# A graph network's projection on TensorE, with its operands swapped: the copied sums held, the weights streamed

## The reference

```python
# layer 0: every edge has 9 coefficients (edge_weight1, edge_attr_3, edge_attr_5)
msg[lo] += einsum('io,eik->eok', W[idx], einsum('ijk,ei,emj->emk', CG[le, ln, lo], sh[le], feats[ln]))
x = x + segment_sum(msg, dst)
# layer 1: 16 bases per edge, weighted by its relation and an attention value, and a self loop
x_hat, y_hat = h[src] @ A1_w.T + A1_b, h[dst] @ A2_w.T + A2_b + rel_emb[etype]
a = tanh(relu(sum(x_hat * y_hat, -1) / sqrt(32)))
msg = einsum('eb,ebo->eo', w_comp[etype], einsum('ei,bio->ebo', h[src], weight))
curr = h[src[last_e]] @ self_loop_weight
x = x + relu(where(in_deg > 0, segment_sum(a * msg, dst) + curr, 0))
```

## Time and profile before

| | us |
|---|---|
| median of 3 runs | 3294.89 |
| lowest and highest | 3294.35, 3296.32 |
| the profiled execution | 3295.84 |
| its span on the core | 3294.0 |
| PE busy in the span | 2972.4 |
| DVE busy | 2602.5 |
| POOL busy | 2414.9 |
| PE's weight loads busy | 2392.0 |
| ACT busy | 895.1 |

### The profile page before, as it was taken

The page is one execution under the profiler, slowest core; times in us unless marked ns, Lnnn a source line. Parts: engine busy times, 40 slices in busy tenths (PEclk is TensorE's granted clock), DMA queues, the critical chain, the costliest instruction groups (busy, mean ns, idle before and its releaser), DMA issues.

```text
span 3294.0 us, 108331 instructions
## 1 busy us (share of the span) xinstructions
PE 2972.4 (90%) x41934; PEld 2392.0 (73%) x41934; DVE 2602.5 (79%) x3897; ACT 895.1 (27%) x1910; POOL 2414.9 (73%) x2546
## 2 busy tenths in 40 slices
PE   2999999999999999999789999999999999899997
PEld 2777777777777777777677777777777777777776
DVE  7777777777777777777678888888888888888886
ACT  1111111111111111111344444444444444444342
POOL 6777777777777777777377777777777777777774
PEclk9999999999999999999789999999999999999998
DMA  4111111111111111111233333333333333332331
GB/s 138 28 28 28 28 28 28 27 28 27 28 27 29 27 29 27 29 27 29 67 55 58 55 59 59 57 56 59 58 57 56 59 58 58 55 58 54 58 57 40
DMA packets 220288, 150.94 MB, mean 46 GB/s; under 512 B 122954, under 2 KB 201083, under 8 KB 219901
## 3 DMA queue, kind: packets, MB, share of 16 engines
q0 software_dynamic: 81312, 41.79, 12.3%
q1 hardware_dynamic: 138013, 100.79, 12.3%
q10 hardware_dynamic: 576, 2.40, 0.2%
HBM read 136.54 MB, written 8.22 MB: 44 GB/s over the span
## 4 chain that ended last, share of the span: by engine, by line
PE 32%; POOL 9%; issue 5%; DVE 4%; DVEq 1%; DMA 0%; ACT 0%; POOLq 0%; ACTq 0%
PE ps L609 17%; POOL xg L541 9%; PE ps L634 5%; PE ps L675 4%; PE ps L622 3%; DVE scratch L960 2%; PE ps L657 1%; PE ps L572 1%; PE ps L645 1%; DVE Z L1044 0%; DMA xg<-h_table,idx 0%; DVE aggT L1062 0%; DVEq L960 0%; DVE blocks L951 0%; DVEq L1062 0%
## 5 line engine op out<-in xcount | busy, mean ns | idle before, releaser
L541 POOL DMA_INDIRECT xg<-h_table,idx x2541 | 2404.1, 946 | 844.1 <-issue 758.9
L609 PE MATMUL ps<-h,blocks 128*128 128x448 f32 x8190 | 1803.0, 372 | 237.5 <-DVE scratch L960 213.4
L609 PEld LDWEIGHTS ps<-h,blocks 128*128 128x128 f32 x8190 | 1501.3, 188 | 458.5 <-issue 324.1
L1044 DVE TENSOR_TENSOR Z<-coef,ps 128x864 f32<-128x864 f32 (+1 forms) x522 | 734.4, 1448 | 16.6 <-DVE ps L985 0.2
L951 DVE TENSOR_TENSOR blocks<-scratch,ps 128x896 fp32r<-128x896 int16 x585 | 630.1, 1077 | 34.4 <-PE ps L609 34.4
L675 PE MATMUL ps<-Z,xg 128*32 128x32 f32 (+3 forms) x25008 | 507.8, 215 | 8.3 <-DVE Z L1044 7.9
L675 PEld LDWEIGHTS ps<-Z,xg 128*32 128x32 f32 x25008 | 403.9, 110 | 93.0 <-issue 70.2
L1062 DVE TENSOR_TENSOR aggT<-aggT,ps 64x128 f32 (+1 forms) x262 | 74.1, 283 | 485.1 <-PE ps L657 478.4
L960 DVE SCALAR_TENSOR_TENSOR scratch<-ramp_sb,scratch,ps 128x448 f32<-128x448 f32 x585 | 396.7, 678 | 7.8
L830 ACT ACTIVATE p_left<-ps 96x128 f32<-96x128 f32 (+2 forms) x262 | 64.6, 246 | 1189.3 <-PE ps L645 1140.8
L965 DVE TENSOR_REDUCE xg<-scratch 128x32 f32<-128x448 f32 x585 | 362.8, 620 | 20.2
(11 more groups left out here) (105 smaller groups left out, 1109.4 us busy)
## 6 DMA issues: line engine op xcount, KB each, us to landing
xg<-h_table,idx POOLq DMA_INDIRECT x2541
rows_b<-typ_short SPq DMA_DIRECT2D x130, 258.0 KB
scratch<-q_short SPq DMA_DIRECT2D x260, 96.0 KB
rows_b<-dst_short SPq DMA_DIRECT2D x130, 126.0 KB
coef<-in_edge_dram SPq DMA_DIRECT2D x130, 54.0 KB
att_tab<-p_table SPq DMA_DIRECT2D x393, 8.1 KB
p_table<-Z SPq DMA_DIRECT2D x8, 297.0 KB, 3.9
X<-in_x_dram SPq DMA_DIRECT2D x7, 224.0 KB, 4.6
```

The lines of the kernel that those rows point to most:

```text
L541: pool.indirect_dma_start(xg[:, g.q, t - g.s * J, :], None, h_table[n], bass.IndirectOffsetOnAxis(ap=idx[:, t:t + 1], axis=0)).then_inc(L. ...
L609: last = pe.matmul(found_ps[b], blocks[:, b, c, :], h_2[:, a, c], start=(c == 0 and a == 0), stop=(c == NCH - 1 and a == 1))
L1044: dve.tensor_tensor(Z[:, b, js, 0:C * WN].rearrange("p j (c n) -> p j c n", n=WN), coef[:, js, :].unsqueeze(3).broadcast_to([P, k, C, WN]) ...
```

## The change

The projection swaps its operands. The copied sums `G_sb` of one half, 96 slots wide, now stand in the array, and the weights stream (64 columns in layer 0, 32 in layer 1). The result has slots on partitions at once and goes to `o_ps`. So there is no `turn`, no `oT_ps`, no `copy_oT` and no semaphore for them. Since a half fills the array, the chunks are gone through once per half: 2 x 3 matmuls of 64 columns instead of 3 of 192 in layer 0, 2 x 5 of 32 instead of 5 of 192 in layer 1. On ACT `copy_o` waits for the projection itself, and stands ahead of the attention of gs[1], where the two copies stood behind it. `place_rows` stays after the 8th tile.

```diff
@@ -198,9 +198,8 @@
 
         G_ps = ps[:, 0:2, :]
         ex_ps = ps[:, 2:4, :]
-        oT_ps = ps[0:2 * F, 4, :]
-        o_ps = ps[0:HW, 4, 2 * HW:2 * HW + 4 * F].rearrange("p (h o) -> p h o", h=2)
-        win_ps = ps[0:3 * F, 4, 2 * HW + 4 * F:2 * HW + 4 * F + P]
+        o_ps = ps[0:HW, 4, 0:4 * F].rearrange("p (h o) -> p h o", h=2)
+        win_ps = ps[0:3 * F, 4, 4 * F:4 * F + P]
         found_ps = [ps[:, 5 + b, 0:MC * F].rearrange("p (f m) -> p f m", f=F) for b in range(2)]
         S_ps = ps[:, 7, 0:J * WN].rearrange("p (j n) -> p j n", j=J)
         iota_ps = ps[:, 7, J * WN:J * WN + P]
@@ -295,9 +294,8 @@
         flat = p_left[:].rearrange("p m k -> p (m k)")
         at = 2 * CQ[1] * HW
         G_sb = flat[:, 0:at].rearrange("p (c h w) -> p c h w", c=CQ[1], h=2)
-        oT_sb = flat[0:2 * F, at:at + 2 * HW].rearrange("p (h w) -> p h w", h=2)
-        o_sb = flat[0:HW, at + 2 * HW:at + 2 * HW + 4 * F].rearrange("p (h o) -> p h o", h=2)
-        at += 2 * HW + 4 * F
+        o_sb = flat[0:HW, at:at + 4 * F].rearrange("p (h o) -> p h o", h=2)
+        at += 4 * F
         one_hot = flat[:, at:at + J * P // 2].bitcast(BF16).rearrange("p (j e) -> p j e", e=P)
         q_rows = coef1[:].rearrange("p b j c -> p (b j c)").bitcast(I16)[0:PS, 0:2 * NPM * P]
         span = squares[0:1].rearrange("p b m f -> p (b m f)")[:, 0:NG]
@@ -368,8 +366,6 @@
                 self.summed = sem(f"summed{n}")
                 self.G_set = sem(f"G_set{n}")
                 self.projected = sem(f"projected{n}")
-                self.oT_set = sem(f"oT_set{n}")
-                self.turned = sem(f"turned{n}")
                 self.o_set = sem(f"o_set{n}")
                 self.placed = sem(f"placed{n}")
                 self.added = sem(f"added{n}")
@@ -627,23 +623,14 @@
                     hh, w = g.halves()
 
                     pe.wait_ge(L.G_set, g.order())
-                    wait(pe, L.oT_set, g.order() - 1)
+                    wait(pe, L.o_set, g.order() - 1)
                     wait(pe, L.added, g.order() - 1)
-                    for c in range(cq):
-                        rows = P if c < cq - 1 else F
-                        last = pe.matmul(oT_ps[0:no, 0:hh * w], weights[0:rows, c, :], G_sb[0:rows, c, 0:hh, 0:w],
-                                         start=(c == 0), stop=(c == cq - 1))
+                    for h in range(hh):
+                        for c in range(cq):
+                            rows = P if c < cq - 1 else F
+                            last = pe.matmul(o_ps[0:w, h, 0:no], G_sb[0:rows, c, h, 0:w], weights[0:rows, c, :],
+                                             start=(c == 0), stop=(c == cq - 1))
                     last.then_inc(L.projected, 1)
-
-                def turn(g):
-                    hh, w = g.halves()
-
-                    pe.wait_ge(L.oT_set, g.order())
-                    wait(pe, L.o_set, g.order() - 1)
-                    pe.nop().then_inc(L.turn_go, 1)
-                    for h in range(hh):
-                        last = pe.transpose(o_ps[0:w, h, 0:no], oT_sb[0:no, h, 0:w], ident[0:no, 0:no])
-                    last.then_inc(L.turned, 1)
 
                 def place_rows(g):
 
@@ -678,8 +665,6 @@
                         if j == g.nj - 1:
                             last.then_inc(L.summed, 1)
                         if back and j == min(g.nj, J // 3) - 1:
-                            turn(back)
-                        if back and j == min(g.nj, 2 * J // 3) - 1:
                             place_rows(back)
 
                 def step(gs):
@@ -693,7 +678,6 @@
                     if gs[1]:
                         sum_edges(gs[1], gs[2])
                     elif gs[2]:
-                        turn(gs[2])
                         place_rows(gs[2])
 
                 def one_pass(k):
@@ -816,16 +800,9 @@
                     act.activation(to[0:F, :, cq - 1, :], bank[0:F, :, cq - 1, 0:w], ACT.Copy)
                     act.activation(to[:, :, 0:cq - 1, :], bank[:, :, 0:cq - 1, 0:w], ACT.Copy).then_inc(L.G_set, 1)
 
-                def copy_oT(g):
+                def copy_o(g):
                     hh, w = g.halves()
                     act.wait_ge(L.projected, g.order())
-                    wait(act, L.turned, g.order() - 1)
-                    act.activation(oT_sb[0:no, 0:hh, 0:w], oT_ps[0:no, 0:hh * w].rearrange("p (h w) -> p h w", h=hh),
-                                   ACT.Copy).then_inc(L.oT_set, 1)
-
-                def copy_o(g):
-                    hh, w = g.halves()
-                    act.wait_ge(L.turned, g.order())
                     wait(act, L.placed, g.order() - 1)
                     act.activation(o_sb[0:w, 0:hh, 0:no], o_ps[0:w, 0:hh, 0:no], ACT.Copy).then_inc(L.o_set, 1)
 
@@ -834,11 +811,10 @@
                         copy_G(gs[2])
                     if n == 1 and gs[0]:
                         one_hots(gs[0])
+                    if gs[2]:
+                        copy_o(gs[2])
                     if n == 1 and gs[1]:
                         attention(gs[1])
-                    if gs[2]:
-                        copy_oT(gs[2])
-                        copy_o(gs[2])
 
                 def one_pass(k):
                     if n == 1 and not isinstance(k, int):
```

## The result

The changed kernel takes 3283.41 us (median of 7, 3282.56 to 3285.16) where the kernel before takes 3295.35 (7 runs), a ratio of 0.9965, 95% interval 0.9953 to 0.9976. Forecast were 3276.4 us, with 3271 to 3297 as range and "faster" as the likeliest side. It is faster, clear of the noise, by 0.35%. The profiled execution took 3283.14 us, its span 3281.3.

What follows compares the result with a forecast made beforehand. PE's loop was taken to end layer 0, POOL's gathers layer 1. From the profiled 3295.84 us, −17.5 (layer 0) and −1 (layer 1's tail) give 3277.3; less 0.95 to the median, 3276.4, range 3271 to 3297.

Steps and rivals of the forecast that it cites:

- The projection: PE's swapped projection between the finds: 1.48 us after 1.35 in layer 0 (+0.13), 2.04 after 1.94 in layer 1.
- (1): The change of array shape at the projection's entry isn't saved: layer 0 −13 us, layer 1 +6, total 3287; chance 0.15.
- (2): Each load in the wide array shape adds some 0.015 us: layer 0 about −17, layer 1 +15, total 3292; chance 0.12.
- Rival (3): A projection load longer than its stream doesn't overlap it: layer 0 +22 us, layer 1 +40, total 3355; chance 0.09.
- The saving of layer 0's loop: PE's loop in layer 0: projection +0.13, turn −0.36, wait for copy_o −0.04, together −0.27 us a group.
- The cap: Layer 0's end: PE's faster loop runs into POOL's gathers, so the layer gains 17.5 us instead of 35.
- Rival (4): POOL was the bound of layer 0 all along, so nothing moves: 3294 us; chance 0.04.
- its two terms: At layer 0's end: the last full group's sums start 15.8 us earlier, and what follows shrinks by 1.7 us.
- Layer 1: Layer 1's new loop through copy_o and attention takes 12.15 us, under the 12.27 limit, so the layer changes by 0.
- Rival (5): Layer 1's new loop is longer by something else, 0.05 to 0.2 us above the limit: 3290 to 3310; chance 0.10.
- its example: In layer 1, R moves with Z and holds up the placing, lengthening the new loop.
- The transition and the tails: After layer 0 its gain carries through; layer 1's tail gives about −1 us: two turns and an ACT trip less, longer projection.

## Why the prediction was right, and where not

**The projection: right.** Loads of 96 columns stand 81 to 85 ns apart (forecast 82), the first is hidden, the change of shape at 128 to 32 rows costs what was worked out: 1.50 us against 1.48 in layer 0, 2404.86 − 2402.79 = 2.07 against 2.04 in layer 1. Rivals (1) and (2) fall with that. Rival (3) falls by the row itself: 20 loads take 2.23 us and run beside the streams, and no row group changes among most of them. So here too the trace contradicts what the prediction took from the Trainium skill (TensorE: Matmul & The Clock Gate, The mechanism), that a load overlaps a running matmul only when the row group differs.

**The saving of layer 0's loop: too small by half.** Forecast 0.27 us a group, measured 0.56 (11.80 to 11.24). PE's steps, start to start, averaged over the groups between 200 and 580 us, say where it comes from. From the first find to the second, with the projection between, they take 0.16 more (forecast 0.13), and the second find 0.02. From the sums to the next first find they take 0.75 less. Of that, 0.36 are the turn and the wait for copy_o (forecast 0.40), and 0.39 are a shorter wait for DVE, 0.77 to 0.38. So the forecast's own terms come to −0.18, and what it put at nothing to −0.39. The step that failed is a misread diff: the placing was held to stay behind the 8th tile. On chip 14 the wait stays at 0.77 us without the early placing, with the swapped projection as with the old (79.3 us in 103 waits there), and falls to 0.43 with it; that the whole 0.39 of the comparison is the placing's is argued from this. None of it made a difference to the time, because of the next step.

**The cap: right.** The gathers end layer 0. PE caught up near group 50, and the last add starts 8.3 us after POOL's last gather does (27.4 before). In the forecast's measure, from that gather's end to the add's, it is 7.7 us (forecast about 9, before 26.8). Rival (4) falls: 18.3 us were gained. That this is so near the forecast's 17.5 is partly luck, since its two terms miss in opposite directions. The sums of the last full group start 14.9 us earlier (1594.53 to 1579.62, forecast 15.8), and what follows up to the last add is 3.4 us shorter (12.94 to 9.59, forecast 1.7). The granted clock differs over that stretch as well: half speed from 1594.4 us on before; after, half from 1572.7, full from 1583.0, half again from 1586.4. Without the cap the saving of layer 0 would have been some 73 us, an estimate (130 x 0.56).

**Layer 1: right where it was asked.** Forecast 12.15 against a limit of 12.27, measured 12.20, pace unchanged. Rival (5) falls; its example was no possible one, since R of the group that is placed was made a step earlier. The misread placing didn't decide here either, by an estimate: in the kernel after, the add starts 1.01 us after the placing's last matmul, where 0.14 is the least seen, and four more tiles of sums ahead of the placing take 0.67. The prediction called copy_o ahead of the attention the place that decides, with 0.12 us to spare. It then priced it only in the running loop, and only with the projection's length. At the end of layer 1 the same link costs 2.07 us of PE's time. On the slow chips it is 3 to 8 us long, and takes the whole gain.

**The transition and the tails: the sum had −1, measured +5.6.** The forecast took the gain of layer 0 through to the end unchanged, and −1 for layer 1's tail, where it counted turns and a trip to ACT that go and not the attention that now waits. What stood behind layer 0 gave back 2.5 us (the stop of the transposes, cause open), 1.5 (POOL's pace, within what traces of one kernel differ by) and 1.6 (ACT's order). For the profiled executions that closes: −0.8 in layer 0, +5.6 and +1 are the 5.8 us between 3277.3 and 3283.14. The other 1.2 of the 7 us between 3276.4 and 3283.4 are where the two profiled executions lie, 0.95 above their median before and 0.27 below it after.

## What to carry to other kernels

Before a saving is multiplied by its count, ask where the next engine's queue ends: here 0.56 us a group were worth 0.14. A change that shortens one chain may put its waiting instruction in front of another chain's on a shared engine; keep the one that depends on a long wait last in the queue. In this kernel that costs nothing in the running loop where semaphores come at once, some 2 us at the end of the layer, and more than the whole gain where they come late. And read a moved call by its line in the diff, not by its name.

The version with the attention first and fewer gathers is the fastest complete kernel of its batch (0.9807 of before, the changed one 0.9996), and the attention first alone had 0.9814 in another batch. Neither was measured where the kernel before takes 3295 us.

## What the runs showed of the hardware

- The same program took 3295 us in the comparison and 4926 to 5013 (medians) on chips 12 and 14, with 2541 gathers of the same 1.25 us in both. On the slow chips the semaphore of the projection came 8.1 us after its end with all gathers and 3.2 us without four a group (medians of the changed kernel in layer 1); the comparison shows 0.01 us. The waits that end with it are put down to "remote" in the rows above. Single instructions of SP and PE came 0.69 us apart, those of ACT, DVE and POOL did not.
- Leaving out 4 of the 9 or 10 gathers of a group gave 0.75 of the time of the kernel before (0.69 in the kernel before itself), though POOL had been waiting for PE in each group, not PE for POOL.
- In the kernel after, PE stops for about 1.5 us ahead of its sums in every second group or so of layer 0 from group 50 on. There its granted clock has short stretches at half speed, from 975.4, 1023.2 and 1071.0 us and two later ones, where the kernel before stays at full speed up to 1594.4. Near the layer's end PE stands still for 8.00 us, until 1579.62, for a gather, and the clock is at half speed from 1572.7 to 1582.9.
- Loads of 96 columns go one behind the other every 81 to 85 ns beside streams of 64 and 32 columns. Ahead of the first there is no idle time, where tiles of 64 and 32 columns had 0.30.
